# High and low parts of q, k and v made once, where they are produced, and 64 attention steps written out

## What is computed

```
Q, K = text @ Wq.T + bq, features @ Wk.T + bk                 # layer 0
attended = softmax(Q @ K.T / sqrt(1024)) @ features
q = apply_rope((query @ wq) as 32 heads of 128)                # layer 1
k = apply_rope((ctx @ wk) as 8 heads of 128);  v = (ctx @ wv) as 8 heads
attn = softmax(q @ k.T / sqrt(128) + mask)                     # 112 x 375 for each head
out = (attn @ v) for all 32 heads, side by side, @ wo
```

## Time and profile before

| | |
|---|---|
| runs shown | 1967.67, 1972.32, 1980.11 us (median 1972.32) |
| span of the profiled execution | 1970.4 us; its own time is not listed apart from the runs; the median lies 1.9 us above this span |
| PE busy | 1869.6 us, 95% |
| DVE, ACT, POOL busy | 57%, 32%, 32% |
| DMA | 188.70 MB, 96 GB/s in the mean |

### The profile page before, as it was taken

One profiled execution on the slowest core, in us unless ns is written; L12 is line 12 of the kernel. 1 busy time (PEld: TensorE's weight loads), 2 busy tenths in 40 slices (PEclk: granted clock), 3 DMA queues, 4 the chain that ended last, 5 costly groups with the idle time before them and its releaser, 6 DMA issues. The chain is left out here.

```text
span 1970.4 us, 30192 instructions
## 1 busy us (share of the span) xinstructions
PE 1869.6 (95%) x9628; PEld 1676.1 (85%) x9628; DVE 1116.1 (57%) x2473; ACT 630.0 (32%) x1337; POOL 623.7 (32%) x427
## 2 busy tenths in 40 slices
PE   5999999998999999979999997899999999999997
PEld 5998999996777777769999987898898989889985
DVE  6631556563222222246666657877777777777766
ACT  2212211022222222221111114565555656565612
POOL 2324522144222222022222233442534434343413
PEclk9999999998999999989999998999999999999998
DMA  3112433245333333222333243232222323232403
GB/s 119 57 61 80 142 99 110 78 135 171 112 113 114 112 113 114 80 76 80 101 104 102 102 140 108 72 100 70 86 72 80 94 65 105 61 91 75 133 3 101
DMA packets 137953, 188.70 MB, mean 96 GB/s; under 512 B 41320, under 2 KB 107432, under 8 KB 137872
## 3 DMA queue, kind: packets, MB, share of 16 engines
q1 hardware_dynamic: 137872, 187.80, 31.1%
HBM read 141.14 MB, written 46.63 MB: 95 GB/s over the span
## 5 line engine op out<-in xcount | busy, mean ns | idle before, releaser
L202 PE MATMUL bank<-shared_operand_high,w_first_high 128*128 128x448 f32 (+1 forms) x768 | 279.4, 364 | 14.7 <-issue 4.9
L202 PE MATMUL bank<-shared_operand_low,w_first_high 128*128 128x448 f32 (+1 forms) x768 | 278.7, 363 | 0.0
L202 PE MATMUL bank<-shared_operand_high,w_first_low 128*128 128x448 f32 (+1 forms) x768 | 278.6, 363 | 0.0
L1354 ACT ACTIVATE e_scores<-e_scores,e_nmax 112x375 f32<-112x375 f32 x256 | 155.1, 610 | 154.9 <-DVE e_nmax L1347 154.3
L202 PE MATMUL bank<-e_o_t_high,e_wo_high 128*128 128x448 f32 x512 | 195.4, 382 | 1.3 <-DVE e_o_t_low L1532 1.3
L202 PE MATMUL bank<-e_o_t_high,e_wo_low 128*128 128x448 f32 x512 | 189.2, 369 | 0.0
L202 PE MATMUL bank<-e_o_t_low,e_wo_high 128*128 128x448 f32 x512 | 188.9, 369 | 0.0
L279 POOL TENSOR_TENSOR shared_operand_low<-ctx_raw,shared_operand_high 128x752 fp32r<-128x752 f32 x64 | 116.3, 1830 | 207.0 <-ACT shared_operand_high L275 207.0
L202 PEld LDWEIGHTS bank<-shared_operand_high,w_first_high 128*128 128x128 f32 x768 | 145.8, 190 | 26.8 <-issue 5.4
L1343 DVE CUSTOM_DVE_ANT_0 e_scores<-bank,e_mask 112x375 f32<-112x375 f32 x256 | 139.8, 546 | 40.8 <-issue 23.0
L1324 POOL TENSOR_TENSOR e_v_low<-e_raw_v,e_v_high 125x384 fp32r<-125x384 f32 x64 | 65.5, 1023 | 287.7 <-ACT e_v_high L1313 287.7
(11 more groups left out here) (173 smaller groups left out, 4185.5 us busy)
## 6 DMA issues: line engine op xcount, KB each, us to landing
ctx_raw<-in_ctx_t SPq DMA_DIRECT2D x64, 376.0 KB, 3.6
e_raw_wo<-in_wo SPq DMA_DIRECT2D x32, 512.0 KB, 5.2
aw_weights_then_ctx_rows<-in_wq SPq DMA_DIRECT2D x30, 512.0 KB, 3.5
q_rotated<-q_rotated_then_x_rows SPq DMA_DIRECT2D x64, 224.0 KB, 1.9
e_raw_q<-q_rotated SPq DMA_DIRECT2D x64, 224.0 KB, 2.8
k_rotated<-k_rotated_sb SPq DMA_DIRECT2D x64, 188.0 KB, 1.9
e_raw_k<-k_rotated SPq DMA_DIRECT2D x64, 188.0 KB, 2.7
aw_weights_then_ctx_rows<-in_ctx_nat SPq DMA_DIRECT2D x8, 1500.0 KB
```

What stands on the lines that cost most here:

```text
L202: mm = pe.matmul(out, stationary[a], moving[b], start=(first and i == 0), stop=(last and i == 2))
L1354: act.activation(self.s_buf[:, t, h, :], self.s_buf[:, t, h, :], ACT.Exp, bias=self.nm[:, t, h:h + 1], accum_out=self.total[:, t, h:h + 1] ...
```

## The change

- **Written out.** All 64 steps stand in the code one after the other; the loop is gone.
- **k** (`key_phase`). DVE's addition writes one of two slots (before: four). ACT makes the high part and POOL the low part, side by side, in one of two slots of `k_parts`, and one DMA stores both (376 KB instead of 188 KB). ACT and POOL each get eight more operations of 128x376 a batch, which stand in their lists among the four tiles of the next context. SP loads context tiles 0 and 1, stores head 0, loads tiles 2 and 3, stores heads 1 to 7. In the last batch the low parts of the seven value-weight tiles are DVE's (before: POOL's), one behind each rotated head.
- **v** (`layer0_phase`). ACT's copy of a piece is its high part; DVE makes the low part (`rows_low`); one store of 500 KB takes both (before 250 KB), and PE's next piece waits for the low part.
- **q** (`query1_phase`). As with k: two slots behind DVE's addition, high part by ACT, low part by POOL, one store of 448 KB (before 224 KB) for each of the 64 units. `first.load` is spread over three pairs of heads.
- **The attention steps** load the parts as they are: 448 KB of q, 376 KB of k, 375 KB of v for each step, straight into the operands. ACT's three copies and POOL's three subtractions a step are gone. q and k are requested two steps ahead (before three), and the request waits for `scored` of the step that used the slot before; v stays two steps ahead. `load_wo` is issued one step ahead, before the request for v. PE waits for the DMAs themselves.

```diff
-    kt_dram = nc.dram_tensor("k_rotated", (BATCH, GROUPS, P, KEYS_EVEN), F32, kind="Internal").ap()
-    v_dram = nc.dram_tensor("v_rows", (BATCH, KEY_TILES, KEY_TILE, DIM), F32, kind="Internal").ap()
-    q_dram = nc.dram_tensor("q_rotated", (HEADS, P, TOK), F32, kind="Internal").ap()
+    kt_dram = nc.dram_tensor("k_rotated", (BATCH, GROUPS, P, 2, KEYS_EVEN), F32, kind="Internal").ap()
+    v_dram = nc.dram_tensor("v_rows", (BATCH, GROUPS, KEY_TILE, KEY_TILES, 2, P), F32, kind="Internal").ap()
+    q_dram = nc.dram_tensor("q_rotated", (HEADS, P, BATCH, 2, SEQ), F32, kind="Internal").ap()
...
             def store_head(b, g):
-                sp.wait_ge(ready, GROUPS * b + g + 3)
-                sp.dma_start(k.kt_dram[b, g], rotated[:, g % 4]).then_inc(stored[g % 4], 16)
...
+                sp.wait_ge(key_low, GROUPS * b + g + 3)
+                sp.dma_start(k.kt_dram[b, g], f32(parts[:, g % 2])).then_inc(stored[g % 2], 16)
...
+            def batch(b, source):
+                load_ctx(b + 1, source, (0, 1))
+                store(b, (0,))
+                load_ctx(b + 1, source, (2, 3))
+                store(b, range(1, GROUPS))
...
             for c in range(3):
                 load_wv(c)
-            store(BATCH - 2)
+            store(LAST, (0,))
             load_ctx(BATCH, 0, (2, 3))
-            for g in range(GROUPS):
-                store_head(BATCH - 1, g)
-                if g + 3 < CH:
-                    load_wv(g + 3)
+            for g in range(1, GROUPS):
+                store_head(LAST, g)
...
+            def head_high(b, g):
+                act.wait_ge(ready, GROUPS * b + g + 3)
+                act.wait_ge(stored[g % 2], 16 * (GROUPS // 2 * b + g // 2) + 16)
+                act.activation(parts[:, g % 2, 0, :], rotated[:, g % 2], ACT.Copy).then_inc(key_high, 1)
...
+                last = known(b) and b == LAST
+                act.wait_ge(acc, GROUPS * b + 2 * GROUPS)
+                ctx_high(b, 1 - t, (0, 1))
+                head_high(b, 0)
+                ctx_high(b, 1 - t, (2, 3))
+                if last:
+                    act.activation(k.qp_split[0], k.qp[:, :, 0:SEQ], ACT.Copy).then_inc(q_high, 1)
+                for g in range(GROUPS):
+                    if g:
+                        head_high(b, g)
+                    if last and g < CH - 1:
+                        before = GROUPS // 2 - 1 if g % 3 < 2 else 0
+                        act.wait_ge(w_in[g % 3], 16 * (before + g // 3) + 16)
+                        act.wait_ge(acc, 16 + GROUPS * LAST + g + 1)
+                        act.activation(weight_tile(k, g)[0], k.raw[:, g % 3], ACT.Copy).then_inc(w_high, 1)
...
+            def head_low(b, g):
+                pool.wait_ge(key_high, GROUPS * b + g + 1)
+                pool.tensor_tensor(parts[:, g % 2, 1, :], rotated[:, g % 2], f32(parts[:, g % 2, 0, :]),
+                                   ALU.subtract).then_inc(key_low, 1)
...
+            def value_weight_low(c):
+                high, low = weight_tile(k, c)
+                dve.wait_ge(w_high, GROUPS + c)
+                dve.tensor_tensor(low, k.raw[:, c % 3], f32(high), ALU.subtract).then_inc(w_low, 1)
...
+                    dve.wait_ge(read, n + 9)
+                    dve.wait_ge(key_low, n + 1)
+                    dve.tensor_tensor(rotated[:, g % 2], straight[:, g % 2], crossed[:, g % 2],
+                                      ALU.add).then_inc(ready, 1)
+                    if known(b) and b == LAST and g >= 1:
+                        value_weight_low(g - 1)
+
...
                 def store_v(p):
-                    sp.wait_ge(v_read, 6 * b + p + 3)
+                    sp.wait_ge(v_low, 6 * b + p + 3)
...
+
+                def rows_low(p):
+                    dve.wait_ge(v_high, 6 * b + p + 1)
+                    dve.tensor_tensor(v_out[:, p % 2, :, 1, :], v_rows(p), f32(v_out[:, p % 2, :, 0, :]),
+                                      ALU.subtract).then_inc(v_low, 1)
...
             def store(unit, i, t, h):
-                sp.wait_ge(ready, unit + 3)
-                sp.dma_start(k.q_dram[2 * i + t, :, h * HALF:(h + 1) * HALF],
-                             rotated[:, 2 * t + h]).then_inc(stored[2 * t + h], 16)
+                sp.wait_ge(head_low, unit + 3)
+                sp.dma_start(k.q_dram[2 * i + t, :, h * QUAD:(h + 1) * QUAD],
+                             f32(parts[:, 2 * t + h])).then_inc(stored[2 * t + h], 16)
...
+            for n in range(5):
+                head_pair(LAST - 5 + n, True)
+                if n < 3:
+                    first.load(sp, n)
...
+            def high(unit, i, t, h):
+                act.wait_ge(ready, unit + 3)
+                act.wait_ge(stored[2 * t + h], 16 * i + 16)
+                take_waits(act, k.passed)
+                act.activation(parts[:, 2 * t + h, :, 0, :], by_batch(rotated[:, unit % 2 if known(unit) else h]),
+                               ACT.Copy).then_inc(head_high, 1)
...
@@ -1284,49 +1392,22 @@
 
     def load_qk(self, sp, s, b, g):
         if not (known(s) and s < 2):
-            sp.wait_ge(self.qk_low, 2 * s - 2)
-        sp.dma_start(self.raw_q[:, b % 2], self.k.q_dram[bass.ds(PER_GROUP * g, PER_GROUP), :,
-                                                         b * SEQ:(b + 1) * SEQ].rearrange(
-            "h p t -> p h t")).then_inc(self.q_in[b % 2], 16)
-        sp.dma_start(self.raw_k[:, b % 2], self.k.kt_dram[b, g]).then_inc(self.k_in[b % 2], 16)
+            sp.wait_ge(self.scored, 4 * s - 4)
+        sp.dma_start(f32(self.q_both[:, b % 2]), self.k.q_dram[bass.ds(PER_GROUP * g, PER_GROUP), :, b].rearrange(
+            "h p a t -> p h a t")).then_inc(self.q_in[b % 2], 16)
+        sp.dma_start(f32(self.k_both[:, b % 2]), self.k.kt_dram[b, g]).then_inc(self.k_in[b % 2], 16)
 
...
+    def load(self, sp, n):
+        if n == 2:
+            sp.dma_start(self.mask[:, :, :], self.k.mask.rearrange("b q s -> q b s")).then_inc(self.mask_in, 16)
+        else:
+            self.load_qk(sp, n, n, 0)
+            self.load_v(sp, n, n, 0)
...
+            for s in range(STEPS):
+                step(s, s % BATCH, s // BATCH)
...
+            def load_wo(n):
+                g, b = divmod(n, 4)
+                if n >= 2:
+                    sp.wait_ge(wo_low, n - 1)
+                sp.dma_start(raw_wo[:, n % 2], k.wo1[g, :, :, b * 256:(b + 1) * 256]).then_inc(wo_in[n % 2], 16)
...
+                if s + 2 < STEPS:
+                    first.load_qk(sp, s + 2, (u + 2) % 8, g + (u + 2) // 8)
+                if (u + 1) % 8 < 4 and s + 1 < STEPS:
+                    load_wo(4 * ((s + 1) // 8) + (u + 1) % 8)
+                if s + 2 < STEPS:
...
+            load_wo(0)
...
-                pe.wait_ge(v_low, s + 1)
+                pe.wait_ge(v_in[t], 16 * half_of(s, u) + 16)
```

279 lines of the change are left out of this document (125 added, 154 removed).

## The result

The changed kernel takes 1984.5 us (median of 20 runs, 1971.8 to 1993.3) against 1972.5 us (20 runs of the kernel before): ratio 1.0059, with a 95% interval of 1.0041 to 1.0077. I had forecast 1952 us and a range that ended at 1979. The change costs 12 us instead of gaining 20. The profiled execution took 1982.8 us, its span is 1981.0 us, 10.6 us above that of before.

A forecast was written before the change was run, and what follows sets the result against it. PE, busy 95% of the span, was taken as the bound. Terms -36 - 11 + 21 + 1.8 + 2 + 1.9 = -20.3 us gave span 1950.1; with 1.9 us around it, forecast 1952 us, range 1933 to 1979.

The forecast's parts named there:

- Part 1: Attention steps 4 to 60: writing them out removes six branch-back losses of 6.0 us each, -36 us; bounds -30 and -37.
- the second loss at a boundary: At each loop branch back, after DVE's 4.28 us stall: four divisions take 3.75 us instead of 1.46 beside POOL's subtractions.
- Part 2: Attention steps 0 to 3: with q, k, v split earlier, 33.4 us instead of 44.4, -11 us; bounds -7 and -13.
- Part 3: Key phase: splits and context tiles in one fixed order add lag, so layer 0 starts later, +21 us; bounds +10 and +30.
- The chain of 32 us: Late key-phase batch: loading, splitting tiles and heads, then DVE takes 32 us against PE's 33.2, shedding about 1 us a batch.
- Part 4: Layer 0: behind the last piece, v's low part and a doubled store precede the barrier, +1.8 us; bounds +1 and +4.
- Part 5: Query phase: spread loads stand before weight loads, +2 us (bounds -2.6 and +13), and +1.9 us at its end.
- Part 6: Loads of the attention steps: 1.2 MB a step takes 6 us of 10, so 0 us.
- a sign of being wrong: Attention steps: waits on `e_q`, `e_k` or `e_v` landings would show the prediction wrong.
- Case C: Key phase: doubled stores lengthen landings, each of six batches loses 1 to 3 us, time 1963 to 1980; chance 0.16.
- The rule on code fetch: Attention loop: a branch outside the two blocks at hand forces a fetch, straight code is fetched ahead; term -36 us.
- The one that Part 3 took: Key phase: POOL shares memory interfaces with DVE and contends with its two-operand instructions; collisions are 5 us of the range.

The follow-up runs named there:

- experiment 1: The kernel before with the 64 attention steps written out and nothing else: 1938.3 us, ratio 0.9808.
- experiment 2: The changed kernel with the loop of seven rounds put back, all else changed: 2015.3 us, ratio 1.0227.
- Experiments 4: The changed kernel with four slots instead of two in the key phase and batch 0's next context ahead of head 0: 1965.5 us, ratio 0.9962.
- 11: The changed kernel with only batch 0's next context ahead of head 0 in the key phase, two slots kept: layer 0 starts at 488.6 us (change 489.6).
- 12: The changed kernel with only four slots instead of two in the key phase, order of lists kept: layer 0 starts at 479.5 us (change 489.6).
- experiment 7: The changed kernel with the store of v's last piece behind the next batch's first two context loads in layer 0: 1973.9 us, ratio 1.0004.
- experiment 10: The changed kernel unaltered, profiled a second time: span 1983.7 us; query-phase matmuls every 206.7 ns, where some other profiles have 202.7.
- Experiment 9: The kernel of experiment 1 without POOL's four clearings of `y_t`; the first eight adding steps write it instead: 1941.2 us, ratio 0.9847.

## Why the prediction was wrong, point by point

- **Part 1, written out (-36):** right, -35.2, and it is the whole worth of the change (experiment 1: -34.5 on the span). What the second loss at a boundary was worth by itself is not shown: in experiment 2 it is gone, but the stall in front of it is longer (6.6 us in the mean for 3.8) and the sum the same.
- **Part 2, steps 0 to 3 (-11):** the number is right, -11.1, but partly by luck. The divisions fell as forecast, to 1.39 us in three steps of the four (2.29 in the first). But I had let PE's own 31.5 us set the length; PE was busy for 25.4, at a granted clock of 0.90, and waited 7.0 us for k to land.
- **Part 3, the key phase (+21):** right in its mechanism and within its bounds, short by 6.6. The chain of 32 us against PE's 33.1 was to shed 1 us of lag a batch. It shed less: the first addition of a batch comes 16.4 us behind PE's start at the third batch and 14.3 at the last, where the kernel before has 6.2. The load that opens the last batch's chain is issued at 447.89, not 438.5. Of these 9.4 us, 2.8 are lag (16.1 us behind PE's start of that batch for 13.3). The other 6.6 are PE's own later start, at 431.81, for I had counted the lag from the old start, 425.22, although I let PE end 2.6 us later. The wait at batch 1 was 5.6 for 3, with 1.8 of half clock behind it. The alternation of weights and heads took 22.7 for 21.7. Experiments 4, 11 and 12 show that the two slots make the lag.
- **Part 4, layer 0 (+1.8, bounds +1 and +4):** the step that failed. I costed the low part on DVE, which does have slack, and the last store; that end cost 3.2. I did not cost the same stores in the middle of the phase. There they hold SP's queue and ACT's slots, and the next context's load, which stands behind them on SP's queue, and ACT's list, in order, carry the delay to PE. Measured +12.2, and +18 in the second profile; experiment 7 gives 10 back by moving one store.
- **Part 5, the query phase (+3.9):** the second step that failed. The loop of weight loads fitted, as worked out: no wait before the one at 1159 us. The spread loads cost 8.9 us of waits where the burst had cost 2.6, 6.3 more; +13 was the bound that I had named and not taken. The transition cost 1.9 as forecast, 5 us are the pace of experiment 10, and half clock costs 1.7 more than before. That makes about 15 of the 16.3.
- **Part 6, the loads of the steps (0):** right from step 4 on, where PE never waits for them. In steps 0 to 3 it was wrong: 7.0 us behind `e_k`, which I had listed as a sign of being wrong.
- **The clock, in no term:** I priced every wait at its length. In the change's profile PE also runs at a granted clock of 0.50 behind the waits of 5.56, 2.80 and 6.33 us, though not behind those of 1.21 and 1.41. That added 1.8 us at batch 1 of the key phase, 3.0 in layer 0 and 2.9 at 1186 us.
- **The sum and the range:** -20.3 for +10.6. Each of the three cost terms was low. The largest error, in Part 4, has one reason: I gave stores of twice the size a price at the places where something waits for the store, and none where something waits in line behind it. Part 5 has the same fault with loads ahead of a load. Case C held that thought for the key phase, with 0.16, but drew its upper end from one phase alone. With Parts 4 and 5 at their own unfavourable ends (+4 and +13) and Part 3 at +30 the same working gives 1974, inside the range; it was Part 4's upper bound, +4 for +12.2, that was too low, and the pace of experiment 10 was in no bound.

The Trainium skill bears on Part 4 (DMA: Bandwidth & Descriptors, section Why a DMA increments its semaphore by 16 and not by 1): a DMA is spread over the largest number of engines up to 16 that divides its slowest dimension. The pieces of v have 125 rows, which by that rule use 5 of 16, a share of 0.31. The trace fits: while these stores and a load of 125 rows are under way, the share stays there, and so it does before (0.32 and 125 GB/s from 553 to 559 us).

```profile
582.00:596.00 14.00, 14.00 (x62) 10.07 (x61) 6.96 (x22) 1.15 (x3) 0.55 (x1) 1.00 0.32 118
```

No run here changes the shape, so the rule itself is not tried. The rule on code fetch that Part 1 took from the Trainium skill (Runtime: NRT & Kernel Launch, section Instruction fetch mechanics) holds for what was forecast: with no branch there was no stall. The one that Part 3 took from the Trainium skill (GPSIMD Engine Reference, section Specifications) speaks, as I put it, of instructions of two operands. Experiment 9's rows show divisions held too, which are not of that kind: 4.2 us for four, with POOL's subtractions of 1.0 and 2.4 us beside them, for 1.4 without.

## What to carry to other kernels

Split an edit before costing it: here one line was worth -35 us, and what came with it +45. When a transfer doubles, follow its queue: ask how long its issue holds the queue, what is issued behind it and which engine's list waits for that, not only who waits for the transfer. Price a wait of PE with the half clock that comes with it. Work that hides under a saturated engine costs nothing there; moved to a phase whose lists are fixed and short of slots, it can set the pace.

## What the runs showed of the hardware that I had not expected

- The stall at a branch back was 3.8 us in the mean in the kernel before and 6.6 in experiment 2, where the DMA engines were busier as the branch was taken (0.65 for 0.25). Nearly all of the difference lies before the first packet of kind `instruction` starts; DVE goes on 2.4 to 2.6 us after that in both.
- The issue of a store can hold SP itself: up to 7.40 us for 500 KB of v, where 250 KB held it for 0.33 us at most. The new stores also have smaller packets (23690 under 2 KB in layer 0, 931 before, of 31822 and 14637), and no run parts the size from the packets.
- The same matmuls of 448 columns go at 202.7 or at 206.7 ns with the same code and the same granted clock of 1.00, in 14 profiles, and change from one to the other within an execution.
